# Cross-attention on one core: blocks arranged in pairs, the product in the even one, three tiles of weighted sums and the light piece in the odd one

## What is computed

```
q = _rmsnorm((x @ Wq.T) by heads);  k, v from context @ Wk.T, context @ Wv.T;  k = _rmsnorm(k)
scores = jnp.einsum('bhnd,bhmd->bhnm', q, k) * scale
attn = jax.nn.softmax(scores, axis=-1)
out = jnp.einsum('bhnm,bhmd->bhnd', attn, v)
...
x = _layernorm(x + _L0_xattn_ref(x, ctx_2048, L0_xattn_Wq, L0_xattn_Wk, L0_xattn_Wv), axis=-1)
```

## Time and profile before

| what | value |
|---|---|
| median of 3 runs | 2435.49 us (2433.94 to 2436.59) |
| the profiled execution | 2440.68 us, its span 2438.0 us |
| TensorE, ScalarE, VectorE, GpSimd busy, of the span | 96%, 55%, 55%, 38% |
| granted TensorE clock, mean | 0.993 |
| exponentials, L1110 | 832, 786.8 us busy |
| weighted sums, L1376 | 3328 rows, 414.7 us busy |
| scores, L1367 | 1664 matmuls, 285.6 us busy |

### The profile page before, as it was taken

How to read it: one execution, slowest core, us unless ns; L and a number is a source line. 1 busy time by engine, 2 the same in 40 slices (tenths; PEclk the granted TensorE clock), 3 DMA queues, 4 the chain that set the end, 5 groups by cost and what they waited for, 6 DMA issues and landing times. The chain is left out here.

```text
span 2438.0 us, 38548 instructions
## 1 busy us (share of the span) xinstructions
PE 2339.3 (96%) x15120; PEld 1504.7 (62%) x15120; DVE 1339.3 (55%) x2102; ACT 1339.6 (55%) x1695; POOL 917.8 (38%) x610
## 2 busy tenths in 40 slices
PE   9999899999999999999999999999899999999998
PEld 8887444444444444444334556665578899898886
DVE  6677434444444434434423656565675577777785
ACT  4332577677766777667896433533522256665222
POOL 2238564555456544555302333333024112221320
PEclk9999999999999999999999999999999999999999
DMA  6003774567546764667653300002035357776431
GB/s 225 18 18 125 215 195 119 152 174 194 126 127 165 203 165 99 164 180 180 169 129 91 122 2 1 18 1 72 18 131 184 114 175 273 251 250 205 154 102 54
DMA packets 205490, 326.68 MB, mean 134 GB/s; under 512 B 71264, under 2 KB 126048, under 8 KB 205152
## 3 DMA queue, kind: packets, MB, share of 16 engines
q1 hardware_dynamic: 185952, 246.51, 36.2%
q0 software_dynamic: 16336, 72.23, 9.0%
q10 hardware_dynamic: 3024, 5.51, 0.7%
HBM read 238.39 MB, written 96.27 MB: 137 GB/s over the span
## 5 line engine op out<-in xcount | busy, mean ns | idle before, releaser
L1110 ACT ACTIVATE A_c_prob<-c_psum 128x1024 f32<-128x1024 f32 x832 | 786.8, 1029 | 281.6 <-PE c_psum L1367 274.7
L1037 POOL TENSOR_TENSOR E_c_roots<-E_c_roots,c_half 128x32 f32<-128x32 f32 (+1 forms) x70 | 363.2, 5191 | 404.6 <-DVE E_c_roots L1127 404.5
L1376 PE MATMUL c_psum<-A_c_prob,c_vq 128*17 128x512 f32 x3328 | 414.7, 598 | 8.6 <-DVE c_oT L1267 8.3
L143 PE MATMUL c_psum<-E_c_w,E_c_c 128*128 128x512 f32 x1248 | 312.6, 400 | 1.6 <-DVEq L1252 0.7
L143 PEld LDWEIGHTS c_psum<-E_c_w,E_c_c 128*128 128x128 f32 x1248 | 226.6, 188 | 122.8 <-issue 41.0
L1367 PE MATMUL c_psum<-c_qq,c_kq 64*128 64x512 f32 x1664 | 285.6, 435 | 15.9 <-ACT A_c_prob L1110 10.0
L1367 PEld LDWEIGHTS c_psum<-c_qq,c_kq 64*128 64x128 f32 x1664 | 135.7, 184 | 158.9 <-ACT A_c_prob L1110 84.2
L1166 DVE COPY E_c_unit<-c_psum 128x256 f32<-128x256 f32 x89 | 37.8, 425 | 328.4 <-PE c_psum L143 328.4
L2766 PE MATMUL m_psum<-A_m_dn_hi,A_m_a 128*128 128x512 f32 (+1 forms) x576 | 187.8, 394 | 3.7 <-DVE A_m_a L2504 3.7
L1376 PEld LDWEIGHTS c_psum<-A_c_prob,c_vq 128*17 128x17 f32 x3328 | 68.6, 96 | 188.4 <-issue 164.6
L1829 DVE TENSOR_REDUCE U_s_areas<-s_psum 128x4 f32<-128x2048 f32 (+1 forms) x64 | 95.5, 1492 | 150.3 <-PE s_psum L1975 141.1
(11 more groups left out here) (360 smaller groups left out, 3954.3 us busy)
## 6 DMA issues: line engine op xcount, KB each, us to landing
c_kq<-kd SPq DMA_DIRECT2D x248, 208.0 KB, 6.0
kd<-S_c_t SPq DMA_DIRECT2D x96, 256.0 KB, 3.9
E_c_raw<-in_ctxT SPq DMA_DIRECT2D x89, 256.0 KB, 4.3
qd<-A_c_q SPq DMA_DIRECT2D x64, 256.0 KB
c_qq<-qd SPq DMA_DIRECT2D x64, 256.0 KB, 3.2
vd<-A_c_vt SPq DMA_DIRECT2D x104, 136.0 KB, 3.4
c_vq<-vd SPq DMA_DIRECT2D x31, 442.0 KB, 8.8
S_up_raw<-in_sup SPq DMA_DIRECT2D x20, 512.0 KB, 4.8
```

The lines of the kernel that those rows point to most:

```text
L143: mm = pe.matmul(out, a(c), b(c), start=first and i == 0, stop=last and i == len(terms) - 1)
L1037: pool.tensor_tensor(rr[:, unit % RB, 0:n], ms[:, unit % RB, 0:n], half[:, 0:n], ALU.pow).then_inc(s_r, 1)
L1110: act.activation(prob[:, t % PB, 2 * (u % 2):2 * (u % 2) + 2, :], score_banks[u % 3], ACT.Exp, scale=XD ** -0.5).then_inc(s_ex, 1)
L1376: mm = pe.matmul(o_bank[32 * j:32 * j + VW, :], vq[:, q % 2, kt, j, :], prob[:, t % PB, j, :], start=kt == 0, stop=kt == CT - 1)
```

## The change

`Timeline.softmax` now decides the piece before the tiles. An odd block k takes every tile whose units come up to 3k, the block's own first unit (mostly three tiles); an even block with a piece takes none beyond 3k - 3 (mostly no tile), and an even block without a piece takes those up to 3k - 1. Products are let into even blocks. Tiles behind a quad's end wait for the next block where there is no piece to stand between (`until`); where there is one, they come behind it. `ahead_of_fill` says how many tiles stand ahead of the piece.

```
-            ready = [t for t in range(done, self.TILES) if 2 * t + 1 <= 3 * k - 1] if k else []
-            done += len(ready)
-            sums.append(ready)
-            ended = [t // CT for t in ready if t % CT == CT - 1]
-            apart_.append(len(ready) == 2 and ready[1] % CT == 0)
...
-            elif heavy_ready() and (len(ready) < 2 or k >= due[heavy[0]] + 4):
+            elif heavy_ready() and (k % 2 == 0 or k >= due[heavy[0]] + 4):
...
-            elif later and not turns and not heavy and (len(ready) < 2 or second(later[0])) and k >= max(unit_done.values()) + 14:
+            elif later and not turns and not heavy and (k % 2 == 0 or second(later[0])) and k >= max(unit_done.values()) + 14:
                 got = later.pop(0)
+            last = self.UNITS if 3 * k >= self.UNITS else 3 * k if k % 2 else 3 * k - 3 if got else 3 * k - 1
+            ready = [t for t in range(done, self.TILES) if 2 * t + 1 <= last]
+            until = next((i + 1 for i, t in enumerate(ready) if t % CT == CT - 1), len(ready))
+            if not got and k < blocks - 1:
+                ready = ready[:until]
+            ahead.append(len(ready) if k % 2 == 0 else until)
+            done += len(ready)
+            sums.append(ready)
+            ended = [t // CT for t in ready if t % CT == CT - 1]
...
-                if piece is line.fill[7]:
+                if piece is line.fill[6]:
                     norm_root(0)
...
-                for t in line.sums[k][0:1 if line.split_pair[k] else 2]:
+                for t in line.sums[k][:line.ahead_of_fill[k]]:
                     weighted(t)
                 if line.fill[k]:
                     put(line.fill[k])
-                if line.split_pair[k]:
-                    weighted(line.sums[k][1])
+                for t in line.sums[k][line.ahead_of_fill[k]:]:
+                    weighted(t)
```

More of the change, by code:

```diff
@@ L691, in __init__ @@
                 at[p.i if p.i < CrossStart.ROOTS else p.index - 2].normalise.append(p.i)
-        self.sums, self.split_pair, self.fill, self.load_at = self.softmax()
+        self.sums, self.ahead_of_fill, self.fill, self.load_at = self.softmax()
         self.normalise = [[] for _ in self.fill]
@@ L741, in softmax @@
         blocks = -(-self.UNITS // 3)
-        sums, apart_, fill, done_at = [], [], [], {}
+        sums, ahead, fill, done_at = [], [], [], {}
         heavy = [(h, *key) for h in range(1, 2 * B) for key in
@@ L822, in softmax @@
         load_at = {q: max(done_at[q - 2] + 1, keys_at(q) if q % 4 == 0 else 0) for q in range(2, B * self.NQ)}
-        return sums, apart_, fill, load_at
+        return sums, ahead, fill, load_at
 def cross_attention(nc, X, regions, first, begun, ident, d):
```

## The result

The changed kernel takes **2497.16 us** (median of 4 runs, 2493.37 to 2499.09) against 2435.7 us of the kernel before in the same session (4 runs). The ratio is 1.0243, with a 95% interval of 1.0231 to 1.0255: 61.5 us slower in the medians.

The account below looks back on a forecast made before the run. TensorE, busy 96% of the span, was taken to bound the kernel. Terms -13 + 26 + 28 - 2 - 2.7 + 6.6 + 2 = 44.9 us on the profiled 2440.68 gave a median of 2480 us, 1.8% slower; range 2456 to 2502.

Parts of the forecast that it names:

- Groups of sums: In cross-attention, 116 fewer groups of sums at 0.11 us each: 13 us saved, bounds 0 to 26.
- The piece behind a light one: 42 products right behind a full `T` or `X` wait 0.63 us for VectorE to empty the shared bank: 26 us lost.
- Short blocks: Blocks under some 2.85 us on TensorE make it wait for ScalarE's exponentials: 28 us lost, bounds 5 to 40.
- Small terms: Within the stage: 2 us saved on waits for quads' copies, 2.7 us for three `A` pieces leaving its body.
- the step that failed: GpSimd's roots and splits, SyncE's stores and quad loads move by a block at most with their pieces: costed at nothing.
- The end of the stage: Three `A` pieces behind the last sums make copy to next stage 9.8 us, not 3.2: 6.6 us lost, bounds 4 to 9.
- Its clock: After TensorE stands still some 4 us at the stage's end, its lower clock costs about 2 us, bounds 0 to 4.
- the losses did not overlap: Rival: waits for the bank and for exponentials overlap, 9 us slower at the least, half-way 2462 us; chance 0.15.
- The switches are not dearer: Rival: each saved group also saves a dear scores-to-sums switch, 0.60 us, so 57 us more saved, 2423 us; chance 0.04.
- its rival's 46 us: Rival: TensorE's clock also falls behind the 27 short blocks, some 1.7 us each, 46 us more, 2526 us; chance 0.07.

Follow-up runs that it names:

- the 90 added groups: Kernel before with VectorE normalising keys before emptying a product, plus the second tile behind the light piece in two-tile blocks: 2450.75 us, 1.0055.
- the kernel with the `A` pieces in either parity: Changed kernel without the parity condition, so `H` and `A` pieces may also go into odd blocks: 2491.12 us, 1.022.
- The experiment with that one load: Kernel before, with SyncE issuing quad 8's load in block 65 in place of 64: 2442.28 us, 1.002.
- that with the weights: Changed kernel, with SyncE issuing the next stage's weight loads ahead of quad 28's load in block 235: 2494.39 us, 1.0235.
- the three edits: Changed kernel with a tile behind `T` or `X`, tiles in short blocks, next stage's weights ahead of quad 28, and VectorE normalising keys before emptying products: 2454.19 us, 1.0064.

## Why the prediction was right, and where it was not

- *Groups of sums*: right. The traces have 282 groups before and 167 now, so 12.7 us at 0.11. (The first row of the account can't show that price, since it is worked out with it: 12.7, 2.7 for the `A` pieces, and 0.87 for a third tile that now stands behind the last unit.) What shows it are the rows, three tiles in 2.70 us, and the 90 added groups at 0.12. A product starts no sooner behind scores, as I had taken it.
- *The piece behind a light one*: right, 30.4 for 26: 43 waits for 42, each 0.69 us from start to start (1.58 less 0.89) for 0.63. Moving a tile behind the `T` in 37 of 42 places gave back what the term says.
- *Short blocks*: right in mechanism, 28.6 us of waits for an exponential and 5.0 of light pieces for the bank, for 28. The row for L1371 grew by only 19.2 us (10.0 to 29.2) because such rows count a wait short. I had forecast 28 for that row without asking from where it counts.
- *Small terms*: the copies of quads, 8.3 us before, are 10.8 now by the rows. Outside block 244 they are 7.6, so 0.7 us are saved where I had forecast 2; that block's 3.21 us belong to the step that failed. Waits of 2.97 (at 300) and 1.83 us are among the rest; before the longest was 1.3. (The 2.97 one stands near where TensorE waited 4.03 us for quad 1's load before; that wait is 1.25 now.)
- *The end of the stage*: right. From the copy to the next stage 8.9 us for 9.8, so 5.7 more than before for 6.6. The table's 6.4 also holds most of the third tile. The chain over VectorE and GpSimd ended it as written, and putting the pieces back took it away.
- *Its clock*: the cost is there, 2.7 us for 2, but a chance of the other trace hides it in the sum. TensorE comes to the same wait for VectorE 12.14 us behind the next stage's first matmul before, and 14.84 now:

```profile
1339.58 0.40 PE L1973 MATMUL s_psum<-s_neg,ident 128*128 128x128 bf16 x4 [1.34 <-DVE U_s_areas L1829]
```

```profile
1400.01 0.40 PE L1977 MATMUL s_psum<-s_neg,ident 128*128 128x128 bf16 x4 [1.33 <-DVE U_s_areas L1833]
```

The wait for VectorE takes nothing off it, and at the 400th matmul of the stage the difference is still 2.6 us (52.93 and 55.54). In the kernel with the `A` pieces in either parity, whose clock does not fall behind the branch, it is 12.11 us to that wait. A little later the kernel before loses more than that. Here are the same 604 matmuls in windows of each (length, PE, PEld, DVE, ACT, POOL busy, clock, DMA share, GB/s), before and now:

```profile
1380.37:1449.24 68.87, 61.29 (x604) 38.83 (x604) 44.19 (x52) 25.56 (x32) 25.22 (x24) 0.93 0.01 2
```

```profile
1440.71:1506.04 65.33, 57.50 (x604) 36.40 (x604) 44.13 (x52) 25.58 (x32) 25.26 (x24) 1.00 0.01 2
```

So from the branch to the end of the span it is 1110.6 us before and 1110.2 now. Over the twelve profiles this stretch, with the same instructions, takes 1104.6 to 1113.4 us. What makes the clock fall there in one execution and not in another stays open.

- *What failed*: the step "GpSimd's roots and splits, SyncE's stores and the quad loads move by a block at most with their pieces ... I cost them at nothing". They moved by one block, and it cost 10.4 us. I had asked how far they move and not how much room each had: quad 8's load takes 14.4 to 14.6 us in three traces, had 14.7 before and 10.5 now. The experiment with that one load gives 5 us in the times and 6.6 in the block; that with the weights gives 4.0 in block 244. The place that I named, a late split of keys holding up a product, was not the one: products waited 2.1 us for GpSimd.
- *The rivals*: the losses did not overlap, since the three edits give nearly the sum of their parts. The switches are not dearer. The clock fell five times in the stage (at 267, 555, 817, 1261 and at its end), once in the kernel before, and not behind each of the short blocks, so its rival's 46 us are not there. But 4.0 us of the loss are more time at the lower level within the stage, which I had at nothing. The Trainium skill (TensorE: Matmul & The Clock Gate, "A second HAM failure mode: psum-queue depth-cycling") lets the clock swing on short idle times between groups, and I had written that the trace does not agree. This trace agrees once, at 267, where no wait is over 1.04 us; over the other waits for an exponential, 73 of 0.8 us at most, it does not.

The median lies 17 us above the 2480 forecast. The two profiled executions differ by 56.8 us (2497.45 less 2440.68), 11.9 more than the terms, of which the two blocks are 10.4. The other 4.9 us are how each stands to its runs: 5.2 us above the median before, 0.3 now. That goes with the clock. The profiled execution of the kernel before had a mean of 0.993. Of its 52 executions beside the experiments, those at 0.993 took 2439.1 to 2441.9 us and those at 0.997 took 2432.4 to 2435.7. That the range still holds the result is in part luck: none of its bounds was made for the two blocks, and they and this offset used up most of its upper side.

## What to carry to other kernels

Where pieces share one PSUM bank, the distance from one piece to the next is a resource: keep more work between them than they need, here 2.1 us from the first transpose to the end of the cast and the subtraction. Larger groups on TensorE save only their entry, 0.11 us here, so they pay only if the blocks left without work are still long enough for the engine that feeds them. When an order is moved "by one block at most", list for each load and each engine in its own order how much room it had, in us, before costing the move at nothing. Count waits of TensorE from start to start; the idle times in its rows came out a third short here (29.2 us for 43.9). And before a stretch is called unchanged, compare the granted clock in it: two executions of the same 604 matmuls were 3.5 us apart, and the clock is the only difference that their windows show.

## What the runs showed of the hardware that was not expected

TensorE's granted clock stayed at its full level over nearly all of some hundred idle times of 0.4 to 0.8 us (0.99 over the stage, where 1.00 is 2.4 GHz). It fell to its lower level (0.50, 1.2 GHz) in or behind the waits of 3.21 us in block 244, 4.07 at quad 8, 3.77 with that load moved and 4.01 at the branch. In the windows behind them its mean is 0.60, 0.72 (6 us), 0.61 (7.5 us) and 0.52. That of block 244:

```profile
1261.00:1263.50 2.50, 2.45 (x12) 0.88 (x12) 0.70 (x2) 0.82 (x1) 0.00 (x0) 0.60 1.01 226
```

Yet a wait of 2.97 us (at 297) left it up, and it fell behind less at two places: behind waits of 0.41, 0.41, 1.04 and 0.37 us within 8 us, and behind one of 1.83:

```profile
265.86 0.41 PE L1340 MATMUL c_psum<-ident,E_c_unit 128*128 128x128 f32 x2 [1.04 <-DVE E_c_unit L1137]
...
267.31 0.50 PE L1371 MATMUL c_psum<-c_qq,c_kq 64*128 64x512 f32 x2 [0.37 <-ACT A_c_prob L1114]
267.74 4.47 PE L1380 MATMUL c_psum<-A_c_prob,c_vq 128*17 128x512 f32 x24
...
817.48 3.39 PE L1380 MATMUL c_psum<-A_c_prob,c_vq 128*17 128x512 f32 x16 [1.83 <-DVE c_oT L1271]
```

Three tiles take 4.40 us there in place of 2.70 and two 3.32 in place of 1.85. Nor does the same wait always do the same. The one at 817 stands in five profiles of the changed order. The clock fell behind it in two and stayed up in three, as in the kernel with the weights first. The wait of 3.52 us for quad 8's load, in the kernel with the `A` pieces in either parity, left the clock at 1.00 too, and its three tiles take 2.70 us:

```profile
815.91 1.91 PE L1380 MATMUL c_psum<-A_c_prob,c_vq 128*17 128x512 f32 x16 [1.85 <-DVE c_oT L1271]
```

```profile
555.28 0.72 PE L1371 MATMUL c_psum<-c_qq,c_kq 64*128 64x512 f32 x4 [3.52 <-DMA c_vq<-vd]
555.93 2.77 PE L1380 MATMUL c_psum<-A_c_prob,c_vq 128*17 128x512 f32 x24
```

So the length of one wait does not tell whether the clock falls. A fall cost 1.5 to 1.8 us in these places, 2.8 with the load moved (6.6 less 3.77) and 2.7 behind the branch.

Changing from one group to another, with row halves for scores, columns for sums and the full array for products, costs little: 0.12 us for a whole added group of sums.
